# Two transformer layers on one core: own memory for the stacks' parts, late constants and zero rows, 24- and 25-row loads, first front reordered, scores for the maxima 13 tiles ahead instead of 16

## What is computed

```python
def _L0_attn_ref(x, Wqkv, Wo):           # D, H, DH = 128, 16, 8
    qkv = (x @ Wqkv).reshape(b, l, 3, H, DH)
    q, k, v = (qkv[:, :, 0], qkv[:, :, 1], qkv[:, :, 2])
    q = q * cos + rotate_half(q) * sin
    k = k * cos + rotate_half(k) * sin
    scores = jnp.einsum('bqhd,bkhd->bhqk', q, k) * DH ** (-0.5)
    attn = jax.nn.softmax(scores, axis=-1)
    out = jnp.einsum('bhqk,bkhd->bqhd', attn, v)
    return out.reshape(b, l, d) @ Wo
...
x = x + _L0_attn_ref(_layernorm(x, axis=-1), ...)
x = x + _L0_ffn_ref(_layernorm(x, axis=-1), ...)   # shared + top 2 of 7 experts
x = x + _L1_attn_ref(_layernorm(x, axis=-1), ...)  # layernorm, qkv with bias, softmax
x = x + _L1_ffn_ref(_layernorm(x, axis=-1), ...)   # relative attention, top 4 of 32 experts
```

## Time and profile before

| | us |
|---|---|
| timed runs | 2059.05, 2066.3, 2070.08 (median 2066.3) |
| profiled execution | 2062.49 |
| its span | 2060.5 |
| busy PE | 1918.0 (93%) |
| busy DVE | 1382.8 (67%) |
| busy ACT | 1205.9 (59%) |
| busy POOL | 507.2 (25%) |

### The profile page before, as it was taken

One profiled execution on the slowest core, in us unless ns is written; L12 is line 12 of the kernel. 1 busy time (PEld: TensorE's weight loads), 2 busy tenths in 40 slices (PEclk: granted clock), 3 DMA queues, 4 the chain that ended last, 5 costly groups with the idle time before them and its releaser, 6 DMA issues.

```text
span 2060.5 us, 40384 instructions
## 1 busy us (share of the span) xinstructions
PE 1918.0 (93%) x13792; PEld 1159.1 (56%) x13792; DVE 1382.8 (67%) x1778; ACT 1205.9 (59%) x2289; POOL 507.2 (25%) x493
## 2 busy tenths in 40 slices
PE   5999999799985999999689999999999999977998
PEld 2333333577762333333356666666666666665887
DVE  6999997556658899996565455555555555346776
ACT  2699999466652799999224444444444444433553
POOL 2000000178862100000222222222222222103654
PEclk8799999899996799999799999999999999988999
DMA  8444542121106445453512211111112211014554
GB/s 275 135 129 127 129 128 77 60 88 63 52 0 196 113 119 134 123 136 86 170 52 60 58 48 50 47 48 47 47 51 61 51 50 47 8 33 179 213 218 144
DMA packets 90189, 198.58 MB, mean 96 GB/s; under 512 B 19872, under 2 KB 49312, under 8 KB 84768
## 3 DMA queue, kind: packets, MB, share of 16 engines
q1 hardware_dynamic: 90080, 197.10, 32.5%
HBM read 162.42 MB, written 36.18 MB: 96 GB/s over the span
## 4 chain that ended last, share of the span: by engine, by line
PE 46%; DVE 2%; DMA 1%; SPq 1%; issue 0%; ACT 0%; DVEq 0%
PE PS L749 17%; PE PS L833 8%; PE PS L761 6%; PE PS L735 6%; PE PS L744 4%; PE PS L724 4%; DVE M L1233 1%; SPq L369 1%; DMA Ks<-in_kv 0%; DMA Ws_r<-w_stack 0%; PE PS L768 0%; PE PS L575 0%; PE PS L707 0%; PE PS L566 0%; PE PS L545 0%
## 5 line engine op out<-in xcount | busy, mean ns | idle before, releaser
L1212 DVE TENSOR_REDUCE M<-PS 128x1 f32<-128x1024 f32 x512 | 595.1, 1217 | 23.0 <-PE PS L630 17.6
L1486 ACT ACTIVATE PR<-PS 128x512 f32<-128x512 f32 x1024 | 539.2, 602 | 41.7 <-PE PS L645 21.3
L1522 ACT ACTIVATE PR<-PS 128x512 f32<-128x512 f32 x512 | 305.8, 598 | 378.5 <-PE PS L749 374.7
L1233 DVE TENSOR_REDUCE M<-PS 128x1 f32<-128x1024 f32 x256 | 311.8, 1221 | 218.4 <-PE PS L735 211.3
L655 PE MATMUL PS<-PR,Va 128*32 128x256 f32 x4096 | 332.2, 397 | 15.6 <-POOL Va L1669 2.7
L645 PE MATMUL PS<-Qs_r,Ks_r 32*128 32x512 f32 x1024 | 310.6, 508 | 0.5 <-ACT PR L1486 0.4
L630 PE MATMUL PS<-Ks_r,Qs_r 32*128 32x512 f32 x1024 | 269.6, 524 | 23.0 <-DVE M L1212 10.3
L630 PEld LDWEIGHTS PS<-Ks_r,Qs_r 32*128 32x128 f32 x1024 | 99.6, 192 | 228.4 <-issue 153.2
L1228 DVE TENSOR_TENSOR rt<-PS,rel 128x512 f32<-128x512 f32 x128 | 88.4, 691 | 162.5 <-PE PS L707 160.9
L655 PEld LDWEIGHTS PS<-PR,Va 128*32 128x32 f32 x4096 | 83.5, 108 | 149.7 <-ACT PR L1486 62.0
L1669 POOL TENSOR_TENSOR Va<-Vt,nil 128x64 f32<-128x64 f32 x96 | 27.8, 293 | 536.7 <-PE PS L655 533.3
(11 more groups left out here) (204 smaller groups left out, 3034.8 us busy)
## 6 DMA issues: line engine op xcount, KB each, us to landing
Qs_r<-q_stack SPq DMA_DIRECT2D x384, 128.0 KB, 2.6
Ks_r<-k_stack SPq DMA_DIRECT2D x384, 128.0 KB, 3.1
Qs<-g_dram SPq DMA_DIRECT2D x29, 1024.0 KB, 4.7
o_dram<-Ob SPq DMA_DIRECT2D x96, 128.0 KB, 2.0
Ks<-g_dram SPq DMA_DIRECT2D x10, 1024.0 KB, 4.8
q_stack<-hl_r SPq DMA_DIRECT2D x18, 256.0 KB, 3.3
k_stack<-hl_r SPq DMA_DIRECT2D x18, 256.0 KB, 4.1
q_stack<-PR_r SPq DMA_DIRECT2D x18, 256.0 KB, 3.2
```

The lines of the kernel that those rows point to most:

```text
L1212: e.tensor_reduce(M[:, s, qt:qt + 1], PS[:, 2 + 2 * (qt % 2):4 + 2 * (qt % 2), :] .rearrange("p a b -> p (a b)"), AX.X, ALU.max, negate=Tr ...
L1233: e.tensor_reduce(M[:, s, qt:qt + 1], PS[:, bk:bk + 2, :].rearrange("p a b -> p (a b)"), AX.X, ALU.max, negate=True).then_inc(max_done, 1)
L1486: e.activation(PR[:, kt % 4, qh * GW:(qh + 1) * GW], bank(RING[(x + turn) % 3]), ACT.Exp, scale=SCALE).then_inc(exp_done, 1)
L1522: e.activation(PR[:, kt % 4, qh * GW:(qh + 1) * GW], bank(TURN[kt % 2][qh]), ACT.Exp)\
```

## The change

- `HL`: front 0 keeps the parts of each group in its own quarter of `BIG`; front 2 uses `hl`, two quarters of `BIG`, and `hl` again for group 3, which waits for group 0's stores; front 3 stays as it was.
- Constants are loaded by SP near the end of attention 0, the zero rows written in experts 0, with only k's row of ones left in front 0. The waits for constants move to front 1.
- `load_qk` loads 24 rows of q and 25 of k; the matmuls use 24 or 25 rows. Relative attention still uses 32.
- Front 0: PE turns group `g + 1` between the k and the q projection; DVE only multiplies, with a second pair of buffers `rtq`; Pool does both additions and both subtractions; ACT rounds after the copy to `XT`.
- `NEAR = 5`: 8 + 5 tiles of scores come ahead of position 0; position `n` has head `n + 1`'s tiles 5 to 7, then head `n + 2`'s 0 to 4. Transpose, wait and copy of the maxima move from steps 1 and 2 to steps 4 and 5.
- SP issues the loads of heads 0 and 1 before group 2's stores, those of head 2 before group 3's, and waits for the stores only before head 3's loads. ACT no longer waits for them.

```diff
-        hls = [hl0_r, PR_r[:, 0:2, :].rearrange("p a (b t) -> p a b t", b=2)]
+        wide = BIG_r[:].rearrange("p (g a b t) -> p g a b t", g=NG, a=2, b=2)
+        PAIR = [hl0_r, PR_r[:, 0:2, :].rearrange("p a (b t) -> p a b t", b=2)]
+        HL = {0: [wide[:, g] for g in range(NG)],
+              2: [hl0_r, wide[:, 2], wide[:, 3], hl0_r],
+              3: [PAIR[g % 2] for g in range(NG)]}
...
+            e.dma_start(k_stack[:, MROW:MROW + 1, :], A["pad"][1:2, 0:1, 0:L].broadcast_to([NH, 1, L])).then_inc(one_in, 16)
...
-            def load_qk(n, s):
-                for to, of in ((Qs_r, q_stack), (Ks_r, k_stack)):
+            def load_qk(n, s, q_depth=MROW, k_depth=MROW + 1):
+                for to, of, depth in ((Qs_r, q_stack, q_depth), (Ks_r, k_stack, k_depth)):
                     for r in range(4):
-                        e.dma_start(to[r * KR:(r + 1) * KR, s, :].bitcast(F32), of[bass.ds(n, 1)].rearrange("n r t -> (n r) t"))\
-                            .then_inc(qk_in[s], 16)
+                        e.dma_start(to[r * KR:r * KR + depth, s, :].bitcast(F32),
+                                    of[bass.ds(n, 1), 0:depth, :].rearrange("n r t -> (n r) t")).then_inc(qk_in[s], 16)
...
                 max_rows(0, 0)
+                if a < 2:
+                    stored(2 * (a + 1))
                 load(3, 3)
...
                 position(NH - 3, 1, False)
+                if a == 0:
+                    constants()
...
+                    if x == 2:
+                        pads()
...
                         for w, bk in ((2, 3), (3, 4), (0, 1), (1, 2)):
+                            if f == 0 and w == 2:
+                                e.wait_ge(krot_ok, g)
+                            if f == 0 and w == 0:
+                                if g + 1 < NG:
+                                    turn_rows(g + 1)
+                                e.wait_ge(qrot_ok, g)
...
                     for kt in range(QT):
-                        if ahead:
-                            if kt == 0:
+                        if kt < QT - NEAR and n + 1 < NH:
+                            scores(n + 1, (s + 1) % SLOTS, NEAR + kt)
+                        if kt >= QT - NEAR and n + 2 < NH:
+                            if kt == QT - NEAR:
                                 e.wait_ge(qk_in[s2], 128 * (NH // SLOTS * a + block + (s >= 2) + 1))
-                            scores(n + 2, s2, kt)
+                            scores(n + 2, s2, kt - (QT - NEAR))
...
-                        if kt == 2 and rows_next:
+                        if kt == 5 and n + 1 < NH:
                             e.wait_ge(mt_copied, HB + n + 2)
...
-                        if kt == 1 and rows_next:
-                            max_row(n + 1, (s + 1) % SLOTS, alone=first)
+                        if kt == 4 and n + 1 < NH:
+                            max_row(n + 1, (s + 1) % SLOTS)
...
-                    for qt in range(QT):
+                    for qt in range([QT, NEAR][n]):
                         scores(n, n, qt)
...
-                        if x == 4 and rows_next:
+                        if x == 10 and rows_next:
                             max_copy(n + 1, (s + 1) % SLOTS)
...
-                e.wait_ge(c_in, 16 * N_CONST)
-                stacks_stored(a)
+                if a == 0:
+                    e.wait_ge(split_k, NG)
+                    e.wait_ge(split_q, NG)
                 max_copy(0, 0)
```

More of the change, by code:

```diff
@@ L291, in two_layers @@
         GATE_BANK = [3, 5, 1, 2]
+        NEAR = 5
         EARLY = (0, GT * (NG - 1))
@@ L319, in _, with constants, pads @@
             e.dma_start(rope[:], A["rope"]).then_inc(rope_in, 16)
[L320 to L327, removed]
+            def constants():
+                loads = [(w_out[:], A["w_out"]), (cols[:], A["cols"]), (rows[:], A["rows"]),
+                         (w_rt0[:], A["w_rt0"]), (w_rt1[:], A["w_rt1"]),
+                         (w_qkv[:, 1:3, :], A["w_qkv"][:, 1:3, :]), (rel[:], A["rel"][:, 1:3, :])]
+                for dst, src in loads:
+                    e.dma_start(dst, src).then_inc(c_in, 16)
+                assert len(loads) == N_CONST
+            def pads():
+                for d, src, w in ((q_stack, 0, L), (k_stack, 1, L), (w_stack, 0, 2 * P)):
+                    e.dma_start(d[:, MROW:KR, :], A["pad"][src:src + 1, :, 0:w].broadcast_to([NH, KR - MROW, w]))\
+                        .then_inc(pad_in, 16)
+            e.dma_start(k_stack[:, MROW:MROW + 1, :], A["pad"][1:2, 0:1, 0:L].broadcast_to([NH, 1, L])).then_inc(one_in, 16)
             def q_out(a, g):
@@ L481, in front @@
                     if g == 2:
[L483 to L486, removed]
+                        stored(2 * a + 1)
                         if f == 3:
+                            e.wait_ge(pad_in, 16 * 3)
                             e.wait_ge(w_out_ok, 16 * 6)
@@ L577, in spread, with turn_rows @@
                     m.then_inc(spread_ok, 1)
+                def turn_rows(g):
+                    e.wait_ge(xn_ok, 4 * f + g + 1)
+                    if a2 is None:
+                        e.wait_ge(xh_ok, 4 * (f // 4) + g)
+                    if f == 0:
+                        e.wait_ge(xs_ok, g)
+                    for t in range(GT):
+                        m = transpose(PS[:, 0, t * P:(t + 1) * P], xn[:, t, :])
+                    m.then_inc(xT_ok, 1)
+                if f == 1:
+                    e.wait_ge(c_in, 16 * N_CONST)
                 if a is not None:
@@ L589, in front @@
                         spread(3)
-                    e.wait_ge(xn_ok, u + 1)
-                    if a2 is None:
-                        e.wait_ge(xh_ok, 4 * (f // 4) + g)
-                    for t in range(GT):
-                        m = transpose(PS[:, 0, t * P:(t + 1) * P], xn[:, t, :])
-                    m.then_inc(xT_ok, 1)
+                    if f > 0 or g == 0:
+                        turn_rows(g)
                     if g:
@@ L657, in values, with position @@
                     m.then_inc(pv_done, 1)
-                def position(n, block, s, turn, first=False, ahead=True, rows_next=True):
+                def position(n, block, s, turn, first=False):
                     s2 = (s + 2) % SLOTS
@@ L693, in attention @@
                 for n in range(1, NH):
-                    position(n, n // SLOTS, n % SLOTS, n % 3, ahead=n < NH - 2, rows_next=n < NH - 1)
+                    position(n, n // SLOTS, n % SLOTS, n % 3)
                 for kt in range(QT - 3, QT):
@@ L1402, in projected @@
                         else:
-                            e.activation(hls[g % 2][:, 1, 0, :], bank(3), ACT.Copy).then_inc(khi_ok, 1)
+                            e.activation(HL[f][g][:, 1, 0, :], bank(3), ACT.Copy).then_inc(khi_ok, 1)
                         e.wait_ge(proj_ok, pr + 2)
-                        e.wait_ge(stq_out[half], 16 * TERMS * (2 * a2 + g // 2))
+                        if f == 3:
+                            e.wait_ge(stq_out[half], 16 * TERMS * (2 * a2 + g // 2))
+                        elif g == 3:
+                            e.wait_ge(stq_out[0], 16 * TERMS * (2 * a2 + 1))
```

103 lines of the change are left out of this document (60 added, 43 removed).

## The result

| | us |
|---|---|
| before, median of 8 | 2062.95 (2059.05 to 2070.08) |
| the change, median of 8 | 2087.98 (2072.42 to 2111.83) |
| ratio | 1.0095, 95% interval 1.0062 to 1.0128 |
| profiled execution of the change, its span | 2070.7 |

The change is slower where 3 us less were forecast, and lies above the range. (The forecast of 2063 took the median of before for 3.8 above its profiled execution, from three runs; over eight it is 0.5 above. That is small beside the miss.) A ratio is made from runs within 1.5% of a kernel's fastest, medians here are over all of its runs; the scatter of this change is itself part of the effect. Its runs follow TensorE's mean granted clock: 2072.4 us at 0.952, 2088.1 at 0.941, 2111.8 at 0.927. The profiled execution is one of its fastest, so it shows 10.2 us of the 25.

The account below looks back on a forecast made before the run. TensorE, 93% busy, was taken to bound the kernel; 0 (front) - 4.6 - 1.8 (starts) + 3 (late rows) + 0.5 (constants) + 0 = -2.9, giving 2063 us as median. Range 2049 to 2082: rival 2 below, rival 1's mild form above.

Parts of the forecast that it names:

- The part on these loads: Loads of 24 and 25 rows: a quarter fewer bytes could save 3 us per attention start; taken as nothing.
- Rival 3: Half-clock spells at attention starts: one position shorter or longer, 4.5 us either way; chance within 0.57 shared with forecast and no-effect.
- Rival 1: Loads of 24 and 25 rows crowd on few DMA engines: 9 us more per start, 2081 as median; chance 0.22.
- Its bound for a tie: Start of attention: crowded loads decide from packets above 0.16 us, where the start ties with the present one.
- Position 0: Starts of attentions 0 and 1: 4.6 us earlier (0 to 8.7) and 1.8 us earlier (0 to 6).
- L: Theory naming Rival 1's mechanism: loads of 25 rows crowd on few DMA engines, 5 of 16.
- Front 0: Reordered front before attention 0: stores land at 35.0 instead of 35.6, 0.6 us earlier; counted 0 in the sum.
- Steady state: Positions mid-attention stay at 9.39 us, set by ACT's sum: net 0, with 10 us either way over 62 positions.
- The deadline: Each position: maxima copy ready 6.8 us in, leaving 2.6 for the row to land; 2.5 taken, 2.8 would cost 12 us.
- Late rows: Mid-attention: instruction fetches delay the maxima row for about 9 of 62 heads, at up to 0.6; 3 us, of 0 to 9.
- Late constants and zero rows: Constants ahead of attention 0's last two maxima rows: 0.5 us, of 0 to 2; zero rows in experts 0: 0.
- Rival 2: Mid-attention exponentials close up toward DVE's 9.05 us per position: 2052.5 or 2042; chance 0.21 together with the smaller loads.

Follow-up runs that it names:

- the pair that isolates it: The change with 32-row matmuls, 24/25-row loads mid-attention; first loads of 32 rows, or in attention 0 of 24 and 25: 2059.9 and 2063.2 us.
- the best version: The change with 32-row loads and matmuls, the maxima's transpose and wait a step earlier, their copy after eight exponentials: 2048.7 us, ratio 0.9931 to before.

## Why the prediction was wrong, step by step

- **The step that failed is the one that isn't in the sum: 24 and 25 rows in the matmuls.** The part on these loads weighs bytes and issues; the matmuls of fewer rows were costed at nothing, without a row for it. They cost 12.6 us alone in the kernel before, and 30 us in the changed one (2089.0 with them, 2058.6 without; 25 by the ratios), as time at half clock: the matmuls themselves are no slower.
- **Rival 3 had the right place and the wrong size and cause.** I took the length of a half-clock spell as chance, one position of 4.5 us either way. A position costs 14.33 at half clock against 9.40, so 4.9, but the profiled execution had about two positions more of it at the start of attention 1 (9.5 us), and 3.3 more behind the late row at 960. Nothing in the change was asked for what the clock might answer to.
- **Rival 1 gave 2081 and was near by luck.** Its mechanism exists: from the first load to the first score the change takes 9.0 us in both starts, 32-row loads 6.7. But it was priced at 9 us a start, as if three heads' loads ran one after another on the busiest engines; the pair that isolates it shows 2.8 at the first score and 4.7 at position 0, the change itself 2.3 at either in attention 0. Its bound for a tie, packets of 0.16 us, doesn't come out of its own counts: 36 more packets on the busiest engines use up 4.6 us at 0.13. Issues cost less, not more, than the 0.37 taken:

```profile
L385 SPq DMA_DIRECT2D Qs_r<-q_stack x100: 303/313/1083, 100.4 to 328.1; - x100
...
L385 SPq DMA_DIRECT2D Ks_r<-k_stack x100: 262/263/264, 102.1 to 329.6; - x100
```

- **Position 0**: 59.5 and 669.1 forecast, 61.3 and 670.1 measured. 2.8 and 0.8 off instead of 4.6 and 1.8, in the bounds; what was missing, 1.8 and 1.0, is no more than L's delay of the first score, 2.3, and may be that.
- **Front 0**: first load at 35.0 forecast, 35.47 measured. Right in this execution, and partly luck: of the nine profiled executions with this front 0, four have the first load at 35.4 to 35.5 and five at 37.8 to 38.2, the unedited change with its copy a step earlier among them (38.21). Those with the old front have it at 35.0 to 35.7. Two of the late ones next to the change show why: PE is at half clock from 21.6 to 25.0 in one and from 19.6 to 26.4 in another, while the change is at full clock there. The reordered front leans on PE between its products, and gains nothing on the whole.
- **Steady state**: 9.39 forecast; the change has 9.40 (copies at 106.96, 116.36 and 125.76). The deadline was met: the row lands 2.50 after its copy in most positions. Right.
- **Late rows**: 3 us, of 0 to 9, forecast. Seven positions are longer, by 3.8 in all, of which the positions behind them give back 0.1 to 0.2 each. Right in itself, but one of them at 960 was followed by 10 us at half clock, which the sum didn't have; and taking the late rows away moved the ratio from 0.9970 to 0.9931 with 32 rows, and from 1.0095 to 1.0062 without (intervals that overlap).
- **Late constants and zero rows**: 0.5 forecast; the position of head 29 to 30 in attention 0, beside the constants, is 0.4 longer and is one of the seven. Nothing waits for either. Right.
- **Rival 2**: no positions of 9.2 anywhere at full clock but behind one that was late or at half clock, as before has them too. It didn't happen.
- **The range**: its upper end, 2082, was the mild form of a rival with the wrong mechanism. An edit without a row for its price should have widened it.

## What to carry to other kernels

Rows that hold zeros were not free to leave out here: ask of every edit to a matmul, its rows too, what it does to the spells at half clock, and time it alone, with enough runs to see the scatter. When a wait is moved to the edge of its room, move what it depends on too; here one step earlier was free, and worth some 4 us in the traces and 8 to 10 in the times. A start that is made earlier may be given back to a stall or to a half-clock spell.

## What was not expected of the hardware

- TensorE at half clock (1.2 GHz) with no idle time of its own: 25.00 of 25 us in the change, 120.00 of 120 with 8-row scores. In these stretches busy time as the profile counts it did not bring the clock back; the number of rows goes with the mean clock (32 rows: 0.952 to 0.965; the change: 0.927 to 0.952; 8 rows in the scores: 0.877 to 0.949). The Trainium skill (TensorE: Matmul & The Clock Gate, "Part 1: The HAM clock gate") says that a unit watches how busy the engine is and sets the clock by it. The fall behind the wait at 960 agrees; that the engine stays at half clock while it is busy throughout does not follow from it, and there the measurement decides. How rows enter wasn't shown: whether it is the weights, the columns that stream past them or what the rows hold was not taken apart. 24 and 25 rows against 32 are told apart, 8 against 24 are not.
- The same program scatters by 39 us (2072 to 2112, 8 runs) with few rows, and by 11 to 18 with many (2044 to 2055 in the best version, 6 runs; 2056.5 to 2074.5 in one batch of 22 of before), and time follows the mean clock.
